# Banded attention stream: value projection moved ahead of the probability transposes

## The chip, the cores and the metric

The kernel runs on one core of one Trainium2 chip. The metric is device time in microseconds (us), lower is better. Four engines compute: TensorE (PE in the rows; PEld are its weight loads), VectorE (DVE), ScalarE (ACT) and GpSimd (POOL); SyncE (SP) issues transfers. Each takes its own instructions in the order in which they are written; between engines only semaphores make one wait for another. TensorE writes its results into eight banks of a memory called PSUM, and VectorE or ScalarE has to move them out before a bank can be written again.

## The reference, cut to what matters

The program is a chain of sixteen layers of different kinds on 2048 tokens of 128 features. The change lies in one of them, which the program runs twice with a retention stage between: a transformer of depth 2 with attention in a band of 64 tokens.

```python
def _layer(x, wqkv, qs, ksc, wo, lg, lb, w1, b1, w2, b2):
    h = shift_token(x)
    q, k, v = jnp.split(h @ wqkv, 3, axis=-1)          # 8 heads of 64
    q = l2norm(q) * qs
    k = l2norm(k) * ksc
    q, k = rotary_xpos(q, k)
    o = local_attention(q, k, v)                        # softmax over a band
    x = x + o @ wo
    h = shift_token(x)
    h = layer_norm(h) * lg + lb
    a, g = jnp.split(h @ w1 + b1, 2, axis=-1)
    x = x + (a * gelu(g)) @ w2 + b2
```

## The kernel before, in words

All values are 32-bit floats. A tile is 128 tokens; the 2048 tokens make 16 tiles, and with two layers the stage handles N = 32 tiles, numbered through. Four tiles make a block of 512 tokens, on which the layer norm and the gated MLP work; there are 8 blocks.

The stage is a software pipeline written out by hand. Each engine has one loop over slots `i = 0, 1, 2, ...`, and in slot `i` several tiles are served, each at another step. On TensorE, slot `i` holds in this order: `turn_qk(i-2)` (L880, 8 transposes of the rotated queries and keys), `project_qk(i)` (L833), an early piece of the MLP or norm (`early`, L943 to L963), `scores(i-2)` (L894 for even tiles, L900 for odd), `project_out(i-4)` (L933), in one slot of four `mean(b)` (L943), `turn_p(i-3)` (L911, 8 transposes of the softmax probabilities in two halves), `project_v(i)` (L868), a late piece of the MLP (`late`), and `values(i-3)` (L926, probabilities times values). The pieces of the MLP go round with r = (i - 8) mod 4, from slot 8 on: r = 0 holds the mean and two `hidden` pieces of the block before, r = 1 the variance and `mlp_out` (L969, three matmuls), r = 2 and r = 3 the gates (L957) and a `hidden` piece (L963). In the first slots, 3 to 7, there is no late piece, and in slots 8 and 9 none either, since no block before exists.

Each output has its PSUM bank: `project_v`, `mean`, `var` and some pieces of the MLP share bank B_V (2); `turn_qk` and `turn_p` share the two banks B_T; the scores have the banks B_S; `values` and `project_out` share B_O.

What the moved calls wait for and who waits for them:

- `turn_p(k)` waits until GpSimd has scaled the probabilities (`p_scaled`, L1142) and ScalarE has emptied B_T (`qk_moved`). ScalarE's `move_p` (L1073, two copies of 128x512) waits for it, and `values` waits for these copies.
- `project_v(k)` waits until bank B_V is free: for VectorE's copy of the tile before (`v_copied`, L1179), and for what the piece of this slot left there. In r = 0 that is `centre` (L1240), VectorE's subtraction of the mean; in r = 2 and r = 3 a ScalarE pass on the gate (L1091, L1099). Its own result is fetched by VectorE (`move_v`, L1179) only in the next slot.
- ScalarE's order in a slot is: `exps(i-3, 1)` (L1063), `move_qk(i-2)` (L1052, L1055), `inverse(i-1)` (L1043, L1045), `square(i)` (L1033), a piece of the norm or the gate (in r = 3 the gelu with two loads of a function table, L1099 to L1103), `move_p(i-3)`, `exps(i-2, 0)`. `scores` waits for `move_qk`, through `window_kt` (L1055).

Of the kernel before, what the change touches and what calls it, by code (L numbers as in the profile page):

```python
# [60 lines left out]
def toks(j, w=W):  # L61
    return slice(j * w, (j + 1) * w)
# [647 lines left out]
def window_attention_stage(K, tag):  # L710
# [4 lines left out]
    N, BLOCKS = DEPTH * TILES, DEPTH * NJ  # L715
# [59 lines left out]
    def part(i):  # L775
        b, r = divmod(i - FIRST, TPW)
        return (b if 0 <= b < BLOCKS else None), (b - 1 if 1 <= b <= BLOCKS else None), r
# [6 lines left out]
    with nc.Block() as block:  # L784
# [35 lines left out]
        def _(pe):  # L820
            def project_qk(k):
                l, j = k // TILES, (k % TILES) // TPW
                if k == 0:
                    pe.wait_ge(st.wa_ready, 16 * DEPTH)
                    pe.wait_ge(outer.norm_ready, 2)
                if k % TPW == 0:
                    pe.wait_ge(sh_ready[j], 32 * (l + 1))
                if k >= 1:
                    pe.wait_ge(st.squared, k)
                    pe.wait_ge(st.cosed, k)  # L830
                    pe.wait_ge(st.sined, 2 * k)
                for a in range(2):
                    mm = nc.tensor.matmul(K.ps[:, B_Q + a, :], sh[:, tok(k)], w_qkv(l, a), start=True, stop=True)  # L833
                mm.then_inc(st.qk_ready, 1)

            def early_moved(i):
                b, last, r = part(i)
                if r == 0 and last is not None:
                    pe.wait_ge(st.hid_done, 3 * last + 2)
                if r == 1 and b is not None:  # L840
                    pe.wait_ge(st.log_ready, b + 1)
                if r >= 2 and b is not None:
                    pe.wait_ge(st.g_moved, 3 * b + 2 * r - 3)

            def mean_moved(i):
                b, last, r = part(i)
                if r == 0 and b is not None:
                    pe.wait_ge(st.centered, b + 1)
# [12 lines left out]
            def project_v(k):  # L861
                if k == 0:
                    pe.wait_ge(outer.norm_ready, 3)
                if k >= 1:
                    pe.wait_ge(st.v_copied, k)
                early_moved(k)
                mean_moved(k)
                nc.tensor.matmul(K.ps[:, B_V, :], sh[:, tok(k)], w_qkv(k // TILES, 2), start=True, stop=True)\  # L868
                    .then_inc(st.v_ready, 1)

            def turn_qk(k):
                if k == 0:
                    pe.wait_ge(outer.log_ready, NJ)
                    pe.wait_ge(outer.norm_ready, NJ)
                pe.wait_ge(st.k_scaled, k + 1)
                if k >= 1:
                    pe.wait_ge(st.pt_copied, 2 * (k - 1))
                for a in range(2):
                    for c in range(QC):
                        mm = nc.tensor.transpose(K.ps[:, B_T + a, toks(c, P)],  # L880
                                                 pa[:, k % 2, a, 2 * c:2 * c + 2, :].rearrange("p h d -> p (h d)"), K.ident)
                    mm.then_inc(st.qk_turned, 1)

            def scores(k):
                pe.wait_ge(st.qk_moved, 2 * (k + 1))
                if k >= 1:
                    pe.wait_ge(st.masked, 2 * k)
                late_moved(k + 1)
                q, keys = (k // 2) % 2, kt[:, (k // 2) % 2]
                for c in range(QC):  # L890
                    if k % 2 == 0:
                        for e in range(2):
                            rows = slice(64 * e, 64 * e + 64)
                            mm = nc.tensor.matmul(K.ps[:, B_S + e, toks(c, P)], qt[rows, c, :], keys[rows, c, 0:P],  # L894
                                                  start=True, stop=True)
                    else:
                        for e in range(2):
                            for u in range(2):
                                rows, own = slice(64 * e, 64 * e + 64), slice(64 * u, 64 * u + 64)
                                mm = nc.tensor.matmul(K.ps[own, B_S + e, toks(c, P)], qt[rows, c, own],  # L900
                                                      keys[rows, c, 64 + 64 * u:64 + 64 * u + P], start=True, stop=True)
                mm.then_inc(st.sim_ready, 1)

            def turn_p(k):
                for e in range(2):
                    pe.wait_ge(st.p_scaled, 2 * k + e + 1)
                    if e == 0:
                        last = min(k + 1, N - 1)
                        pe.wait_ge(st.qk_moved, 2 * (last + 1))
                    for c in range(QC):  # L910
                        mm = nc.tensor.transpose(K.ps[:, B_T + e, toks(c, P)], s[:, k % 2, e, c, :], K.ident)  # L911
                    mm.then_inc(st.pt_ready, 1)
# [17 lines left out]
            def project_out(k):  # L930
                pe.wait_ge(st.o_moved, k + 1)
                for c in range(QC):
                    mm = nc.tensor.matmul(K.ps[:, B_O, 0:P], w_out(k // TILES, c), of[:, c, :],  # L933
                                          start=(c == 0), stop=(c == QC - 1))
                mm.then_inc(st.proj_ready, 1)

            def mean(b):
                l, j = divmod(b, NJ)
                if b < BLOCKS - 1:
                    pe.wait_ge(sh2_ready[j], 32 * (l + 1))  # L940
                else:
                    pe.wait_ge(st.y_attn, N)
                nc.tensor.matmul(K.ps[:, B_V, :], K.mean_mat, sh2[:, toks(j)], start=True, stop=True)\  # L943
                    .then_inc(st.mean_ready, 1)
# [28 lines left out]
            def early(i):  # L973
                b, last, r = part(i)
                pe.wait_ge(st.v_copied, up_to(i))
                if i > N:
                    early_moved(i - 1)
                    mean_moved(i - 1)
                if r == 0 and last is not None:
                    hidden(last, 1)  # L980
                if r == 1 and b is not None:
                    var(b)
                if r == 2 and b is not None:
                    gate(b, 0)
                if r == 3 and b is not None:
                    gate(b, 2)

            def late(i):
                b, last, r = part(i)
                pe.wait_ge(st.masked, up_to(2 * (i - 2) + 1, 2 * N))  # L990
                if i > N + 1:
                    late_moved(i - 1)
                if r == 0 and last is not None:
                    hidden(last, 2)
                if r == 1 and last is not None:
                    mlp_out(last)
                if r == 2 and b is not None:
                    gate(b, 1)
                if r == 3 and b is not None:
                    hidden(b, 0)  # L1000

            outer.pe(pe, 0, K.x, lambda j: None)
            for i in stream:
                b, last, r = part(i)
                if 2 <= i < N + 2:
                    turn_qk(i - 2)
                if i < N:
                    project_qk(i)
                if i >= FIRST:
                    early(i)  # L1010
                if 2 <= i < N + 2:
                    scores(i - 2)
                if 4 <= i < N + 4:
                    project_out(i - 4)
                if r == 0 and b is not None:
                    early_moved(i)
                    mean(b)
                if 3 <= i < N + 3:
                    turn_p(i - 3)
                if i < N:  # L1020
                    project_v(i)
                if i >= FIRST:
                    late(i)
                if 3 <= i < N + 3:
                    values(i - 3)
# [3033 lines left out]
```

## Time and profile before

| | us |
|---|---|
| runs | 2560.93, 2563.16, 2550.03 (median 2560.93) |
| profiled execution | 2562.57 |
| span of the profile | 2560.8 |
| busy in the span: PE | 2188.4 (85%) |
| DVE | 1711.1 (67%) |
| ACT | 1431.7 (56%) |
| POOL | 716.6 (28%) |

The two banded attention stages lie at about 391 to 757 us (first projection to last piece of the MLP) and at about 813 to 1178 us. The shares above are means over sixteen stages with different limits; what this change does has to be read inside these two.

### The profile page before, as it was taken

Reading aid. Unit: us, or ns where it says so; the run is one execution under the profiler, and the core shown is the slowest. Engines: PE = TensorE matmul, PEld = TensorE weight load, DVE = VectorE, ACT = ScalarE, POOL = GpSimd, SP = SyncE. Lnnn points to the kernel's source line nnn. Section 1 sums busy time; section 2 is a strip of 40 time slices with the busy share of each in tenths; the row PEclk is TensorE's granted clock in tenths of the full one; section 3 lists DMA queues with packets and bytes.
Section 4 is the critical chain, followed back from the end, with each engine's and each line's share of the span. In section 5 each row is a group of like instructions: output and inputs, shape, how many; then the busy total and the mean of one; then the engine's idle time right before and its main releaser. Section 6 shows DMA issues by size and latency. Waiting matters only on the chain. (4 is left out here: it accounts for less than half of the span.)

```text
span 2560.8 us, 43202 instructions
## 1 busy us (share of the span) xinstructions
PE 2188.4 (85%) x15324; PEld 1484.8 (58%) x15324; DVE 1711.1 (67%) x4380; ACT 1431.7 (56%) x3703; POOL 716.6 (28%) x473
## 2 busy tenths in 40 slices
PE   5999997999987999998748888768876989889998
PEld 4788774665644656653547774423423767656657
DVE  6777757887846988873655554356455989547874
ACT  3555646777764887876512215563645756235762
POOL 0000004554511654540133420000011879132000
PEclk9999999999998999999868998988986989888998
DMA  1000002011002010101022220000001212100010
GB/s 59 15 14 20 9 26 63 22 28 24 22 14 79 18 28 20 30 18 51 1 65 56 56 47 4 9 12 7 4 13 42 83 66 75 69 12 1 2 69 18
DMA packets 79492, 81.47 MB, mean 32 GB/s; under 512 B 28688, under 2 KB 64272, under 8 KB 78256
## 3 DMA queue, kind: packets, MB, share of 16 engines
q1 hardware_dynamic: 79280, 78.72, 10.7%
q8 instruction: 124, 2.03, 0.3%
q14 instruction: 88, 0.72, 0.1%
HBM read 53.94 MB, written 8.52 MB: 24 GB/s over the span
## 5 line engine op out<-in xcount | busy, mean ns | idle before, releaser
L1142 POOL TENSOR_TENSOR window_s<-window_s,window_soft 128x512 f32<-128x512 f32 x128 | 132.9, 1039 | 301.2 <-DVE window_soft L1172 301.2
L1232 DVE CUSTOM_DVE_ANT_0 window_s<-ps,window_mask,window_nrn 128x128 f32<-128x128 f32 x512 | 148.5, 346 | 95.6 <-PE ps L900 52.2
L1063 ACT ACTIVATE window_s<-window_s,window_soft 128x128 f32<-128x128 f32 x512 | 197.9, 395 | 2.5 <-DVE window_soft L1232 2.5
L3218 DVE TENSOR_TENSOR_SCAN mamba_bx<-ps,mamba_ab 128x256 f32<-128x256 f32 x256 | 154.6, 667 | 20.4 <-PE ps L3004 20.4
L1150 POOL TENSOR_TENSOR window_pa<-window_pa,window_pb 128x1024 f32<-128x1024 f32 x64 | 151.3, 2364 | 39.0 <-DVE window_pb L1214 39.0
L833 PE MATMUL ps<-window_wa,window_sh 128*128 128x512 f32 x256 | 127.3, 621 | 25.8 <-DVE window_pb L1214 14.1
L3388 ACT ACTIVATE rope_p<-ps,rope_mx 128x128 f32<-128x128 f32 (+1 forms) x256 | 104.1, 418 | 50.5 <-DVE rope_mx L3442 50.4
L3001 PE MATMUL ps<-mamba_m,mamba_xt 128*128 128x129 f32 x512 | 102.9, 283 | 29.7 <-ACT mamba_m L3076 20.6
L1073 ACT ACTIVATE window_pt<-ps 128x512 f32<-128x512 f32 x128 | 69.7, 595 | 85.9 <-PE ps L911 85.8
L3106 POOL TENSOR_TENSOR h<-mamba_bx,mamba_cbr 128x1024 f32<-128x1024 f32 x32 | 89.2, 2792 | 96.3 <-DVE mamba_bx L3218 95.7
L83 PE MATMUL ps<-x,consts 128*128 128x512 f32 x120 | 75.3, 786 | 45.7 <-PEq L53 40.1
L580 POOL TENSOR_TENSOR linattn_y<-linattn_y,linattn_wa 128x512 f32<-128x512 f32 x24 | 28.3, 1179 | 303.2 <-DVE linattn_xn L619 303.2
L3076 ACT ACTIVATE mamba_m<-mamba_step,mamba_b_tm 128x129 f32<-128x129 f32 (+1 forms) x256 | 78.4, 389 | 60.6 <-PE ps L3004 57.0
L3001 PEld LDWEIGHTS ps<-mamba_m,mamba_xt 128*128 128x128 f32 x512 | 82.2, 197 | 49.5 <-issue 49.5
L1933 ACT ACTIVATE delta_ym<-ps 128x512 f32<-128x512 f32 x48 | 28.7, 597 | 130.0 <-PE ps L1739 130.0
L3004 PE MATMUL ps<-mamba_m,mamba_xt 128*128 128x128 f32 x512 | 101.1, 279 | 0.0
L1063 ACT ACTIVATION_READ_ACCUMULATOR window_s<-window_s,window_soft 128x1 f32 x512 | 99.6, 194 | 0.0
L417 PE MATMUL ps<-linattn_h,linattn_wb 128*128 128x512 f32 x192 | 95.9, 604 | 1.8 <-ACT linattn_h L493 1.8
L3106 POOL TENSOR_TENSOR ln_xc<-mamba_bx,mamba_cbr 128x1024 f32<-128x1024 f32 x32 | 90.0, 2813 | 22.3 <-DVE mamba_bx L3218 21.3
L3094 POOL MEMSET mamba_xi<- 128x48 f32 x1 | 0.1, 148 | 342.1 <-POOLq L53 342.1
L426 PE MATMUL ps<-linattn_wb,linattn_hid 128*128 128x128 f32 x768 | 89.7, 275 | 0.0
L426 PEld LDWEIGHTS ps<-linattn_wb,linattn_hid 128*128 128x128 f32 x768 | 87.7, 192 | 0.0
(615 smaller groups left out, 6173.2 us busy)
## 6 DMA issues: line engine op xcount, KB each, us to landing
mamba_cbr<-mamba_c SPq DMA_DIRECT2D x32, 512.0 KB, 3.5
window_vs<-window_vt SPq DMA_DIRECT2D x64, 128.0 KB, 2.3
delta_xi<-delta_x SPq DMA_DIRECT2D x16, 512.0 KB, 4.7
switch_w<-in_switch_w SPq DMA_DIRECT2D x4, 2048.0 KB, 10.0
window_wa<-in_window_wa SPq DMA_DIRECT2D x4, 1152.0 KB, 6.6
linattn_wb<-in_linattn_wb SPq DMA_DIRECT2D x6, 513.0 KB, 3.6
window_wb<-in_window_wb SPq DMA_DIRECT2D x4, 537.5 KB, 7.7
window_sh<-y SPq DMA_DIRECT2D x16, 128.0 KB, 3.7
```

The lines of the kernel that those rows point to most:

```text
L417: nc.tensor.matmul(K.ps[:, B_H + c % 2, :], w1(s, c), h[:, 1, s % 2, :], start=True, stop=True)\
L426: mm = nc.tensor.matmul(K.ps[:, B_O, toks(t, P)], hid[:, s % 2, c, toks(t, P)], w2(s, c), start=(c == 0), stop=(c == CH - 1))
L833: mm = nc.tensor.matmul(K.ps[:, B_Q + a, :], sh[:, tok(k)], w_qkv(l, a), start=True, stop=True)
L1063: a = nc.scalar.activation(s[:, k % 2, e, c, :], s[:, k % 2, e, c, :], ACT.Exp, scale=-1.0, bias=soft[:, k % 2, e, 1, c:c + 1], accum_out= ...
L1142: nc.gpsimd.tensor_tensor(s[:, k % 2, e], s[:, k % 2, e], soft[:, k % 2, e, 3, :].unsqueeze(2).to_broadcast([P, QC, P]), ALU.mult)\
L1150: nc.gpsimd.tensor_tensor(own, own, pb[:, :, :, :].rearrange("p a h d -> p (a h d)"), ALU.add)\
L1232: v = nc.vector.tensor_tensor_reduce(s[:, k % 2, e, c, :], K.ps[:, B_S + e, toks(c, P)], mask[:, k % 2, :], nrn[:, k % 4, h:h + 1], 3e38, ...
L3001: nc.tensor.matmul(out[:, at0:at0 + P + 1], xt[:, TH * H + 2 * q, toks(c, P)], m[:, (k // CC) % 2, 2 * q, :], start=(q % 2 == 0), stop=Fal ...
L3004: mm = nc.tensor.matmul(out[:, at0 + P:at0 + LEN], xt[:, TH * H + 2 * q + 1, toks(c, P)], m[:, (k // CC) % 2, 2 * q + 1, 0:P], start=False ...
L3106: nc.gpsimd.tensor_tensor(cg_buf(k), g_buf(k), cbr[:, (k // CC) % 4, :], ALU.mult).then_inc(st.cg_ready, 1)
L3218: g = nc.vector.tensor_tensor_scan(g_buf(k)[:, LEN * q:LEN * (q + 1)], K.ps[:, v_bank(k) + q // 2, at0:at0 + LEN], a_buf(k)[:, LEN * q:LEN ...
L3388: a = nc.scalar.activation(p[:, n % 2, e, part_of(t)], K.ps[:, 2 * (n % 2) + e, part_of(t)], ACT.Exp, bias=mx[:, n % 4, t, e:e + 1], accum ...
```

## The change

`project_v(i)` and `turn_p(i - 3)` change places in TensorE's loop. Nothing is added or removed, and the other four engines' instructions stand as before. `turn_p` runs in slots 3 to 34 and `project_v` in slots 0 to 31, so the order changes in slots 3 to 31: 29 slots in each of the two stages.

```diff
                 if r == 0 and b is not None:
                     early_moved(i)
                     mean(b)
+                if i < N:
+                    project_v(i)
                 if 3 <= i < N + 3:
                     turn_p(i - 3)
-                if i < N:
-                    project_v(i)
                 if i >= FIRST:
                     late(i)
```

The first place is on TensorE in slot 5 of the first stage, before the MLP has begun. `window_of` is the attended output that `project_out` reads, `window_s` the probabilities, `window_sh` the shifted input, `window_pt` the transposed probabilities. Before:

```order
L900 MATMUL ps<-window_kt,window_qt 64x128 x16
L933 MATMUL ps<-window_of,window_wa 128x128 x4
L911 MATMUL ps<-consts,window_s 128x128 x8
L868 MATMUL ps<-window_wa,window_sh 128x512
L926 MATMUL ps<-window_pt,window_vt 64x128 x8
```

and after:

```order
L900 MATMUL ps<-window_kt,window_qt 64x128 x16
L933 MATMUL ps<-window_of,window_wa 128x128 x4
L868 MATMUL ps<-window_wa,window_sh 128x512
L911 MATMUL ps<-consts,window_s 128x128 x8
L926 MATMUL ps<-window_pt,window_vt 64x128 x8
```

The projection (L868) no longer stands between the transposes (L911) and the product that needs their copies (L926).

The second place is on TensorE in a slot with r = 0, where the mean of a block (L943, of `window_sh2`, which the names show as `window_sh`) goes into bank B_V. Before:

```order
L894 MATMUL ps<-window_kt,window_qt 128x128 x8
L933 MATMUL ps<-window_of,window_wa 128x128 x4
L943 MATMUL ps<-window_sh,consts 128x512
L911 MATMUL ps<-consts,window_s 128x128 x8
L868 MATMUL ps<-window_wa,window_sh 128x512
L963 MATMUL ps<-ln_xc,window_wb 85x512
L926 MATMUL ps<-window_pt,window_vs 64x64 x2
```

and after:

```order
L894 MATMUL ps<-window_kt,window_qt 128x128 x8
L933 MATMUL ps<-window_of,window_wa 128x128 x4
L943 MATMUL ps<-window_sh,consts 128x512
L868 MATMUL ps<-window_wa,window_sh 128x512
L911 MATMUL ps<-consts,window_s 128x128 x8
L963 MATMUL ps<-ln_xc,window_wb 85x512
L926 MATMUL ps<-window_pt,window_vs 64x64 x2
```

The transposes no longer stand between the two matmuls that use bank B_V, L943 and L868.

## Rows read from the trace of the kernel before

**Rows 1.** Page, part 1: busy us, share of the span, instructions.

```profile
PE 2188.4 (85%) x15324; PEld 1484.8 (58%) x15324; DVE 1711.1 (67%) x4380; ACT 1431.7 (56%) x3703; POOL 716.6 (28%) x473
```

**Rows 2.** Busy us by stretch: PE, PEld, DVE, ACT, POOL; granted clock, DMA share, GB/s.

```profile
520.00:560.00 40.00, 37.84 (x325) 24.45 (x322) 32.81 (x111) 31.56 (x99) 19.81 (x15) 1.00 0.09 20
```

**Rows 3.** Waits of PE, 822 to 1140 us: total us, times, longest.

```profile
PE ps L926 <- ACT window_pt L1073: 7.8, 6, 1.3
...
PE ps L943 <- DVE window_hid L1257: 5.1, 6, 0.9
...
PE ps L963 <- DVE window_vt L1179: 0.4, 1, 0.4
PE ps L957 <- DVE window_vt L1179: 0.4, 1, 0.4
```

**Rows 4.** Timeline of PE, one block: start us, us, what, [idle before <-releaser].

```profile
521.50 1.04 PE L911 MATMUL ps<-consts,window_s 128*128 128x128 f32 x8
522.38 1.02 PE L868 MATMUL ps<-window_wa,window_sh 128*128 128x512 f32 x2
523.24 1.02 PE L957 MATMUL ps<-ln_xc,window_wb 128*128 128x512 f32 x2
524.19 0.34 PE L926 MATMUL ps<-window_pt,window_vs 128*64 128x64 f32 x4
...
528.87 1.10 PE L900 MATMUL ps<-window_kt,window_qt 64*64 64x128 f32 x32
...
534.97 1.09 PE L926 MATMUL ps<-window_pt,window_vt 128*64 128x128 f32 x16 [1.30 <-ACT window_pt L1073]
...
542.70 1.13 PE L943 MATMUL ps<-window_sh,consts 128*128 128x512 f32 x2 [0.85 <-DVE window_hid L1257]
543.66 1.04 PE L911 MATMUL ps<-consts,window_s 128*128 128x128 f32 x8
544.71 1.10 PE L868 MATMUL ps<-window_wa,window_sh 128*128 128x512 f32 x2
545.64 1.02 PE L963 MATMUL ps<-ln_xc,window_wb 128*85 128x512 f32 x2
546.59 0.34 PE L926 MATMUL ps<-window_pt,window_vs 128*64 128x64 f32 x4
...
555.04 2.74 PE L969 MATMUL ps<-window_hid,window_wb 128*128 128x512 f32 x6
```

**Rows 5.** Timeline of ACT in the same block, slots r = 2 and r = 3.

```profile
522.14 1.08 ACT L1073 ACTIVATE window_pt<-ps 128x512 f32<-128x512 f32 x2 [1.31 <-PE ps L911]
...
527.23 0.58 ACT L1055 ACTIVATE window_kt<-ps 128x512 f32<-128x512 f32 x1
528.11 0.22 ACT L1043 ACTIVATE window_stat<-window_stat 128x16 f32<-128x16 f32 x1 [0.29 <-DVE window_stat L1188]
...
533.83 1.08 ACT L1073 ACTIVATE window_pt<-ps 128x512 f32<-128x512 f32 x2
```

**Rows 6.** Timeline of DVE in the slot r = 0: the centring.

```profile
543.88 0.68 DVE L1240 TENSOR_TENSOR ln_xc<-window_sh,ps 128x512 f32<-128x512 f32 x1
```

**Rows 7.** Timeline of PE, slots 6 to 8 of the first stage.

```profile
440.77 1.16 PE L894 MATMUL ps<-window_kt,window_qt 64*128 64x128 f32 x16
...
442.86 1.04 PE L911 MATMUL ps<-consts,window_s 128*128 128x128 f32 x8
...
446.02 1.09 PE L880 MATMUL ps<-consts,window_pa 128*128 128x128 f32 x8 [0.18 <-POOL window_pa L1154]
...
448.80 1.10 PE L900 MATMUL ps<-window_kt,window_qt 64*64 64x128 f32 x32
...
461.28 1.10 PE L868 MATMUL ps<-window_wa,window_sh 128*128 128x512 f32 x2 [0.48 <-DVE ln_xc L1240]
```

**Rows 8.** Timeline of ACT, slots 6 and 7 of the first stage.

```profile
443.49 1.08 ACT L1073 ACTIVATE window_pt<-ps 128x512 f32<-128x512 f32 x2 [0.68 <-PE ps L911]
...
448.02 0.58 ACT L1055 ACTIVATE window_kt<-ps 128x512 f32<-128x512 f32 x1
```

## The prediction, made before the changed kernel was run

> **What bounds the kernel now.** I read from wide to narrow. The page's first part has TensorE busy for 85% of the whole span [rows 1], which says little about two stages out of sixteen. The busy time by stretch says more: in the repeating part of the banded stage TensorE works 37.84 of 40 us, at full granted clock (2.4 GHz), while VectorE works 32.81 and ScalarE 31.56 [rows 2]. So TensorE's order is the time there, and whatever makes it stand still is added. The view of waits then says where it stands still already [rows 3]: in six slots `values` waits 1.3 us each for ScalarE's copies of the probabilities (L1073), in six slots the mean waits 0.85 us for VectorE, and only twice, 0.4 us each, does a piece wait for VectorE's copy of the projected values. The wait that the new order could remove, transposes (L911) waiting for GpSimd with a projection idle behind them, has no row in this stretch. The timelines give the distances [rows 4 to 8].
>
> **The change part by part.** Both calls stay, so TensorE's work is the same: a slot of 0.88 us for the transposes (521.50 to 522.38) and 0.86 us for the projection (522.38 to 523.24) [rows 4]. What changes is who stands behind whom. Three things follow.
>
> First, the transposes come 0.86 us later, and with them ScalarE's two copies. From the start of the transposes to the start of the copies it takes 522.14 - 521.50 = 0.64 us, the copies take 1.08, and `values` starts 0.06 behind them (533.83 + 1.08 = 534.91, start at 534.97) [rows 4, 5]. So `values` can't begin earlier than 1.78 us after the transposes begin. Before, the projection and the late piece stood between and covered that: 524.19 - 521.50 = 2.69 us. Now what covers it is the transposes (0.88) and the late piece alone (524.19 - 523.24 = 0.95), together 1.83 us. In a slot with a late piece that is just enough, with 0.05 us left: I take 0 and keep 0 to 0.1. In r = 1 the late piece is `mlp_out` (2.74 us) and covers everything.
>
> Slots 3 to 7 have no late piece. There I follow the round of two engines, from scores to the next scores. Scores to transposes is 442.86 - 440.77 = 2.09 us, transposes to the end of ScalarE's copy of the keys is 448.02 + 0.58 - 442.86 = 5.74 us (copies, eight exponentials and the copies of queries and keys, back to back), and 0.06 for the semaphore: 7.89 us, hidden under a period of 448.80 - 440.77 = 8.03 us that another chain sets, through GpSimd [rows 7, 8]; the 0.18 us that L880 waits for it there is the mark of that. With the projection between scores and transposes the round becomes 7.89 + 0.86 = 8.75 us and sets the period: +0.72 us. Slot 3 still has waits that swallow it; four periods follow, so 4 x 0.72 = 2.9 us. Bounds: 0 if the copies are covered after all, 4 x 0.86 = 3.4 if nothing is.
>
> Second, bank B_V. In r = 0 the mean (L943) and the projection both write it, and VectorE must centre in between. Centring starts at 543.88, directly when VectorE is free, and ends at 544.56; the projection starts at 544.71 [rows 4, 6]. That time is set by VectorE and doesn't move when the projection is put earlier in the queue. Before, the transposes filled it (543.66 to 544.54). Now TensorE stands still from 543.66 to 544.71, and the transposes start at 545.64 behind the projection. They end at 546.52, the late piece at 547.47, against 546.59 for the start of `values` before: +0.88 us. The copies are ready at 545.64 + 1.78 = 547.42, in time. This happens in slots 12, 16, 20, 24 and 28: 5 x 0.88 = 4.4 us. The bounds are 0 (if centring came so much earlier that nothing waits) and 1.05 us each, the whole new gap. Slot 8 is the same without a late piece: the projection starts at 461.28 as before [rows 7], the transposes take the place that `values` had behind it, and `values` comes 1.78 us later. It used to come about 0.1 us after the projection, so I take 1.7 us, between 0.9 and 1.8. In slot 9, also without a late piece, what follows waits 0.40 us for VectorE's copy of the values (L957) [rows 3] behind other VectorE-set starts, so the 0.86 is swallowed there: 0, at most 0.86.
>
> The Trainium skill has a rule against such a neighbourhood: "Perfetto Trace Analysis", section Matmuls, wants independent matmul groups to rotate through different PSUM banks so that the evacuation of one overlaps the next group's matmuls. The new order puts two users of one bank side by side in r = 0 and takes away the group from another bank. By this rule alone only the slots with a mean would pay; the rows agree that they pay and say that others do too.
>
> Third, ScalarE's lateness. In r = 2 its copies start at 522.14 after 1.31 us of idling, and from there to the key copy, which ends at 527.81, nothing is idle; the next gap is 0.29 us before L1043 at 528.11 [rows 5]. Shift it all by 0.86: the key copy ends at 528.67, still before the scores at 528.87 [rows 4], but L1043 and all behind it come 0.86 - 0.29 = 0.57 us later. What follows is the chain of two table loads and gelus, without a gap, up to the copies at 533.83, and these are what `values` waits for in r = 3, 1.30 us now, 1.87 us then. Six slots (11, 15, ..., 31): 6 x 0.57 = 3.4 us; bounds 0 (another gap that I don't see in the chain) and 0.86. The other effect of the order in r = 3 is free: the projection must wait for the gate pass of ScalarE (L1099), but TensorE waits for ScalarE later in that slot anyway.
>
> What the earlier projection itself can win: VectorE fetches it in the next slot and isn't waiting for it, so the most is the two waits for that copy, 0.8 us a stage [rows 3]. I take 0, since VectorE comes to it at its own time.
>
> Sum for one stage: 2.9 + 1.7 + 4.4 + 3.4 = 12.4 us. A delay once made is not won back, as each next step hangs on `values` or `scores`, and the stage ends at a barrier. Twice: 24.8 us. The profiled execution took 2562.57 us, 1.6 us above the median of the three; from there 2587.4, from the median of 2560.93 it is 2585.7. I say 2586.
>
> **The rivals.**
>
> A, only the bank pair costs. The copies are late in no slot that matters, ScalarE catches up before the gelus; left are the six slots with a mean, (4.4 + 1.7) x 2 = 12.2 us, 2573. For it: that gap is the plainest in the rows. Against it: ScalarE's rows show no idle time in which to catch up.
>
> B, every slot pays. If the 0.05 us of cover in slots with a late piece isn't there (`mlp_out` aside), and what is late adds to itself through ScalarE, the bound is 29 x 0.86 x 2 = 50 us, 2611. For it: 0.05 us is less than the rows can promise. Against it: only the missing part of the cover would be paid, not the whole 0.86.
>
> C, not slower, by one mechanism: in r = 3 TensorE waits 1.30 us for ScalarE. If that chain starts from something that doesn't move with TensorE, the 0.88 us lost in r = 0 comes out of this wait instead of being added, and the third part is 0 too. Left is the start, (2.9 + 1.7) x 2 = 9.2 us, 2570, which is within 0.5%; it decides itself at the point where a block's loss is under 1.30 us. With the start swallowed as well it is 2561. Against it: the chain starts at L1043, which waits for VectorE, and VectorE in its turn for the scores of TensorE.
>
> D, faster: the value copies come sooner and the two waits of 0.4 us go, 2 x 0.8 = 1.6 us, 2559; anything more would need a wait of the transposes for GpSimd, and there is none to fill.
>
> **How the numbers follow.** The forecast has 0.62, A 0.12, B 0.06, C 0.16, D 0.04. About 0.5%, or 12.8 us, is what a measurement of this kernel can tell from no change, since its three runs lie 13 us apart. Slower by more than that, above 2573.7: the forecast, B and a part of A, 0.76; within it: the rest of A and C, 0.20; faster 0.04. The forecast's own range is 2575 to 2598 (below, the third part at 0, 6.8 us less, and some of the start; above, 0.86 in the third part and in slot 9, and a part of the cover missing). For 8 in 10 I go down to 2568, which takes in A and a part of C, and up to 2600.
>
> **What the next profile would show.** In r = 0, L943 followed by a gap of about 1 us before L868, released by VectorE's L1240, then L911. In r = 3, the wait of `values` for L1073 near 1.9 us in place of 1.30. In slots 4 to 7, a period near 8.75 us, with PE waiting for `window_kt` (L1055) and no longer for GpSimd. In slot 8, `values` waiting about 0.9 us for L1073. Each block of four slots, from one wait of `values` in r = 3 to the next, would be 0.88 + 0.57 = 1.45 us longer. I am wrong if the block's length doesn't change, if `values` waits in r = 2 as well, or if busy times of single instructions differ.

## The result, and the profile of the changed kernel

The changed kernel takes 2585.11 us (median of 4 runs, 2578.45 to 2594.75), the kernel before, run beside it, 2559.28 us (4 runs, 2550.03 to 2563.16). The ratio is 1.0104 with an interval of 1.0083 to 1.0125: slower by 1.0%. The prediction was 2586. The profiled executions took 2586.16 and 2562.57 us, 23.6 us apart.

The instruction counts are as before, and the busy times nearly so: on TensorE 2195.2 us in place of 2188.4 [rows 1], the other three compute engines within 3.1 us. First the page's first part, then busy time by stretch (PE, PEld, DVE, ACT, POOL, granted clock, DMA share, GB/s), the same 40 us as [rows 2]:

```profile
PE 2195.2 (85%) x15324; PEld 1486.2 (58%) x15324; DVE 1712.0 (66%) x4380; ACT 1428.7 (55%) x3703; POOL 716.2 (28%) x473
```

```profile
520.00:560.00 40.00, 36.73 (x306) 23.02 (x306) 30.52 (x105) 29.26 (x85) 21.76 (x16) 1.00 0.12 28
```

At the same clock TensorE works 36.73 us there, before 37.84. The two windows don't hold the same pieces of a block. Over the whole stretch that is measured at the end of this section (one stage, from slot 4 on) TensorE is busy for 308.7 us of 341.2, before 306.8 of 328.8, at granted clock 1.00 in both: 10.5 us of the 12.4 are standing still. The other 1.9 us are busy time. A pair of 128x512 matmuls is shown as 1.10 us long behind a wait and as 1.02 in the flow, so part of it belongs to the new waits too. Where TensorE stands still, the view of TensorE's waits shows for the second stage, 822 to 1160 us (total us, times, longest):

```profile
PE ps L868 <- ACT window_gl L1099: 6.7, 6, 1.1
...
PE ps L926 <- ACT window_pt L1073: 6.2, 11, 0.7
PE ps L868 <- DVE ln_xc L1240: 5.8, 6, 1.3
...
PE ps L943 <- DVE window_hid L1257: 5.1, 6, 0.9
...
PE ps L894 <- ACT window_kt L1055: 0.5, 2, 0.4
...
PE ps L963 <- DVE window_vt L1179: 0.4, 1, 0.4
PE ps L868 <- ACT window_gl L1091: 0.2, 1, 0.2
```

The projection (L868), which waited once before, for 0.5 us, now waits thirteen times in this list. The list leaves out waits under 0.15 us, and it says where TensorE stood, not what it cost: some of these waits only took the place of others. TensorE's timeline over one block (start us, us, what, [idle before <-releaser]) answers to [rows 4]:

```profile
525.45 1.04 PE L911 MATMUL ps<-consts,window_s 128*128 128x128 f32 x8
526.32 1.02 PE L957 MATMUL ps<-ln_xc,window_wb 128*128 128x512 f32 x2
527.28 0.34 PE L926 MATMUL ps<-window_pt,window_vs 128*64 128x64 f32 x4
...
531.96 1.10 PE L900 MATMUL ps<-window_kt,window_qt 64*64 64x128 f32 x32
...
535.27 1.10 PE L868 MATMUL ps<-window_wa,window_sh 128*128 128x512 f32 x2 [1.11 <-ACT window_gl L1099]
536.20 1.04 PE L911 MATMUL ps<-consts,window_s 128*128 128x128 f32 x8
537.07 1.02 PE L963 MATMUL ps<-ln_xc,window_wb 128*128 128x512 f32 x2
538.52 1.09 PE L926 MATMUL ps<-window_pt,window_vt 128*64 128x128 f32 x16 [0.42 <-ACT window_pt L1073]
...
546.25 1.12 PE L943 MATMUL ps<-window_sh,consts 128*128 128x512 f32 x2 [0.85 <-DVE window_hid L1257]
548.26 1.10 PE L868 MATMUL ps<-window_wa,window_sh 128*128 128x512 f32 x2 [0.89 <-DVE ln_xc L1240]
549.19 1.04 PE L911 MATMUL ps<-consts,window_s 128*128 128x128 f32 x8
550.06 1.02 PE L963 MATMUL ps<-ln_xc,window_wb 128*85 128x512 f32 x2
551.02 0.34 PE L926 MATMUL ps<-window_pt,window_vs 128*64 128x64 f32 x4
...
582.77 1.09 PE L926 MATMUL ps<-window_pt,window_vt 128*64 128x128 f32 x16 [0.42 <-ACT window_pt L1073]
```

The block, from `values` in r = 3 to the next, lasts 582.77 - 538.52 = 44.25 us; before it was 577.89 - 534.97 = 42.92, from the row in [rows 4] to this one:

```profile
577.89 1.09 PE L926 MATMUL ps<-window_pt,window_vt 128*64 128x128 f32 x16 [1.30 <-ACT window_pt L1073]
```

In r = 2 `values` starts 527.28 - 525.45 = 1.83 us after the transposes without waiting: the cover holds. In r = 0 it starts 551.02 - 546.25 = 4.77 us after the mean, before 3.89 [rows 4]. In r = 3 it starts 538.52 - 531.96 = 6.56 us after the scores, before 6.10.

ScalarE's timeline, slots r = 2 and r = 3, answers to [rows 5]:

```profile
526.09 1.09 ACT L1073 ACTIVATE window_pt<-ps 128x512 f32<-128x512 f32 x2 [2.18 <-PE ps L911]
...
531.18 0.59 ACT L1055 ACTIVATE window_kt<-ps 128x512 f32<-128x512 f32 x1
531.66 0.22 ACT L1043 ACTIVATE window_stat<-window_stat 128x16 f32<-128x16 f32 x1
...
537.38 1.08 ACT L1073 ACTIVATE window_pt<-ps 128x512 f32<-128x512 f32 x2
```

L1043 no longer waits for VectorE; it starts 0.30 us before the scores (531.96 - 531.66) in place of 0.76 (528.87 - 528.11). That 0.46 us is what `values` loses in r = 3.

In the first slots TensorE's timeline answers to [rows 7]:

```profile
434.89 1.09 PE L926 MATMUL ps<-window_pt,window_vt 128*64 128x128 f32 x16 [0.74 <-ACT window_pt L1073]
...
438.92 1.16 PE L894 MATMUL ps<-window_kt,window_qt 64*128 64x128 f32 x16 [0.19 <-ACT window_kt L1055]
...
443.65 0.34 PE L926 MATMUL ps<-window_pt,window_vs 128*64 128x64 f32 x4 [0.74 <-ACT window_pt L1073]
...
447.67 1.10 PE L900 MATMUL ps<-window_kt,window_qt 64*64 64x128 f32 x32
...
460.86 1.10 PE L868 MATMUL ps<-window_wa,window_sh 128*128 128x512 f32 x2 [1.34 <-DVE ln_xc L1240]
```

The period is 447.67 - 438.92 = 8.75 us where it was 8.03. L880 no longer waits for GpSimd; the scores of slot 6 wait 0.19 us for the key copy.

For the whole stage I measure from the start of the scores in slot 4 to the start of the last `mlp_out`. In the first stage this is 753.55 - 424.74 = 328.8 us before and 762.71 - 421.48 = 341.2 after, +12.4; in the second it is the same to 0.1 us. Twice 12.4 is 24.8 us. The profiled executions differ by 1.2 us less; that difference lies outside these stretches.

### The profile page after: what moved, and what is told of

Read it like the earlier page. It is cut to its first block and busy times, and to the rows that moved or that the text cites. A ratio compares the mean times of both kernels' runs of the same rounds, so it can differ in the third digit from the quotient of the medians.

```text
span 2584.4 us, 43202 instructions
## 1 busy us (share of the span) xinstructions
PE 2195.2 (85%) x15324; PEld 1486.2 (58%) x15324; DVE 1712.0 (66%) x4380; ACT 1428.7 (55%) x3703; POOL 716.2 (28%) x473
## 5 line engine op out<-in xcount | busy, mean ns | idle before, releaser
L1073 ACT ACTIVATE window_pt<-ps 128x512 f32<-128x512 f32 x128 | 69.7, 595 | 142.4 <-PE ps L911 142.3
L833 PE MATMUL ps<-window_wa,window_sh 128*128 128x512 f32 x256 | 127.1, 621 | 21.8 <-DVE window_pb L1214 12.3
L868 PE MATMUL ps<-window_wa,window_sh 128*128 128x512 f32 x128 | 69.9, 629 | 25.4 <-ACT window_gl L1099 13.4
```

## The experiments

The first six start from the kernel before, the last two from the changed one. The first four were run beside a kernel before of 2556.76 us (median of 25 runs), the last four beside one of 2559.18 (23 runs). One execution of each was profiled, and the rows come from it. Three lines more in the source turn L1073, L1099 and L1240 into L1076, L1102 and L1243 there (in the fifth L1079, L1105 and L1246; in the eighth nothing moves). "Stretch" is slot 4's scores to the last `mlp_out`, 328.8 us before.

**1. New order in r = 0 alone.**

```diff
+                ahead = i >= FIRST and r == 0
+                if i < N and ahead:
+                    project_v(i)
                 if 3 <= i < N + 3:
                     turn_p(i - 3)
-                if i < N:
+                if i < N and not ahead:
                     project_v(i)
```

> The new order only in the slots with r = 0 (slot 8, 12, 16, 20, 24, 28), the old one elsewhere. Theory: the projection waits there for the centring of bank B_V, and nothing behind wins it back. Each block of four slots grows by 0.88 us (from 42.9), slot 8 costs 1.7 us, in all (5 x 0.88 + 1.7) x 2 = 12.2 us over the kernel before; the wait of values for ScalarE's copies in r = 3 stays at 1.30 us. Rival (C of the prediction): the 0.88 us comes out of that wait, which falls to about 0.4 us, the block keeps its length, and only slot 8 costs, 3.4 us in all. Rival: only lateness of ScalarE's copies costs, then the block is unchanged and its wait too.

Measured: 2574.15 us against 2556.76, ratio 1.0073 (1.0052 to 1.0094). In TensorE's timeline the wait in r = 3 stays:

```profile
538.39 1.09 PE L926 MATMUL ps<-window_pt,window_vt 128*64 128x128 f32 x16 [1.30 <-ACT window_pt L1076]
546.11 1.13 PE L943 MATMUL ps<-window_sh,consts 128*128 128x512 f32 x2 [0.85 <-DVE window_hid L1260]
548.13 1.10 PE L868 MATMUL ps<-window_wa,window_sh 128*128 128x512 f32 x2 [0.89 <-DVE ln_xc L1243]
...
582.18 1.09 PE L926 MATMUL ps<-window_pt,window_vt 128*64 128x128 f32 x16 [1.30 <-ACT window_pt L1076]
```

This block lasts 43.79 us, +0.87, and slot 8 costs 1.7 us. Rival C falls: nothing is taken out of the 1.30 us. Four of the ten slots with a mean (12 to 28, in both stages) cost 1.68 us more, and there the timeline looks like this:

```profile
500.64 1.12 PE L943 MATMUL ps<-window_sh,consts 128*128 128x512 f32 x2 [0.85 <-DVE window_hid L1260]
502.65 1.93 PE L868 MATMUL ps<-window_wa,window_sh 128*128 128x512 f32 x2 [0.89 <-DVE ln_xc L1243]
504.38 1.91 PE L911 MATMUL ps<-consts,window_s 128*128 128x128 f32 x8
```

The two matmuls take 1.93 us in place of 1.10. The busy time by stretch has the granted clock (third number from the end) in the same place, where before it was 1.00:

```profile
500.00:510.00 10.00, 8.47 (x57) 5.20 (x58) 7.25 (x19) 4.27 (x17) 2.14 (x3) 0.83 0.00 0
```

This is a mean over 10 us; between 503 and 505 us the same view gives 0.50, which is 1.2 GHz. Together that is 12.2 + 4 x 1.68 = 18.9 us by the trace, 17.4 by the medians. The expectation was right on the mechanism and 5 us short on the whole. In the profiled execution the clock accounts for it. That execution was the slowest of the four (2582.51 us, the others 2572.09 to 2575.54), and what the clock did in the others isn't on record.

**2. New order in slots 3 to 7 alone** (`ahead = 3 <= i < FIRST`).

> The new order only in slots 3 to 7, where no late piece stands between transposes and values. Theory: the round scores, projection, transposes, copies, exponentials, key copy, scores becomes 8.72 to 8.75 us and sets the period in place of 8.03; 4 x 0.7 = 2.8 to 2.9 us a stage, 5.7 us in all; values waits 0.74 us for L1073 in each of these slots and the wait of L880 for GpSimd goes. Rival: the 0.74 us of waiting is only moved from other waits and the period stays at 8.03, 0 us.

Measured: 2562.90 us, ratio 1.0023 (1.0012 to 1.0033), 6.1 us more than before. The periods are 8.75, 8.69, 8.75 and 8.74 us, before 8.03, 8.01, 8.03 and 8.02; the stretch is 331.7 us, +2.9, and blocks stay at 42.92. The round through ScalarE sets the period, as expected.

**3. New order in r = 2 alone** (`ahead = i >= FIRST and r == 2`).

> The new order only in slots with r = 2. Theory: in the slot itself TensorE loses nothing, but ScalarE is about 0.86 us late from its copies on, catches up 0.3 to 0.4 us, and brings the gelus of r = 3 and the copies behind them 0.46 to 0.57 us late: the wait of values in r = 3 grows from 1.30 to 1.76 to 1.87 us, the block by as much, 6 x 0.5 x 2 = 5.5 to 6.8 us in all. Rival: ScalarE catches up before the gelus; the wait stays at 1.30 us, the block at 42.9, 0 us.

Measured: 2566.96 us, ratio 1.0040 (1.0023 to 1.0056). TensorE's timeline in r = 2 and r = 3:

```profile
521.63 1.04 PE L911 MATMUL ps<-consts,window_s 128*128 128x128 f32 x8
522.51 1.02 PE L957 MATMUL ps<-ln_xc,window_wb 128*128 128x512 f32 x2
523.46 0.34 PE L926 MATMUL ps<-window_pt,window_vs 128*64 128x64 f32 x4
...
531.45 1.10 PE L868 MATMUL ps<-window_wa,window_sh 128*128 128x512 f32 x2 [0.24 <-ACT window_gl L1102]
532.38 1.02 PE L963 MATMUL ps<-ln_xc,window_wb 128*128 128x512 f32 x2
534.70 1.09 PE L926 MATMUL ps<-window_pt,window_vt 128*64 128x128 f32 x16 [1.30 <-ACT window_pt L1076]
```

The block is 578.08 - 534.70 = 43.38 us, +0.46. In these slots the order in one slot is paid in the next, in which nothing was changed. The sign I named was wrong: the wait of `values` stays at 1.30 us and the lateness shows in front of the projection, which now waits for L1102. It starts 3.31 us after the scores, before 2.90; the view counts only 0.24 of that as idle. Slot 10 costs 0.44 us of its own and slot 30 another 0.27: their gate pass (L1091) is still running when the projection comes. The stretch is 332.3 us, +3.5, so 7.0 us for both stages. The medians differ by 10.2 us. The ten runs spread from 2560.04 to 2575.61 us, and the profiled one, 2560.50, is near their lower end; what the slower ones did isn't shown.

**4. New order in r = 3 alone** (`ahead = i >= FIRST and r == 3`).

> The new order only in slots with r = 3. In the changed kernel the projection waits 1.11 us there for ScalarE's gate pass (L1099). Theory: that wait costs nothing, since values later in the slot waits for ScalarE in any case; with the new order in r = 3 alone the projection waits about 0.65 us and values about 0.65 us in place of 1.30, the block stays at 42.9 us, 0 us in all. Rival: the wait for L1099 is a cost of its own, 0.6 us or more for each of six slots, 7 us or more in all.

Measured: 2559.34 us, ratio 1.0004 (0.9990 to 1.0018); block 576.61 - 533.69 = 42.92 us, stretch 328.8.

```profile
530.44 1.10 PE L868 MATMUL ps<-window_wa,window_sh 128*128 128x512 f32 x2 [0.65 <-ACT window_gl L1102]
533.69 1.09 PE L926 MATMUL ps<-window_pt,window_vt 128*64 128x128 f32 x16 [0.42 <-ACT window_pt L1076]
```

So 0.65 of the 1.11 us that the projection waits for L1099 in the changed kernel (head of its list, 6.7 us) costs nothing. The other 0.46 is the lateness from r = 2, which the third experiment has shown to cost.

**5. In r = 0: transposes, mean, late piece, projection, values.**

```diff
+                around = i < N and r == 0 and last is not None
+                if around:
+                    turn_p(i - 3)
                 if r == 0 and b is not None:
                     early_moved(i)
                     mean(b)
-                if 3 <= i < N + 3:
+                if around:
+                    late(i)
+                    project_v(i)
+                if 3 <= i < N + 3 and not around:
                     turn_p(i - 3)
-                if i < N:
+                if i < N and not around:
                     project_v(i)
-                if i >= FIRST:
+                if i >= FIRST and not around:
                     late(i)
```

> The kernel before, with another order in slots 12, 16, 20, 24 and 28 alone: transposes, mean, late piece, projection, values, in place of mean, transposes, projection, late piece, values. Theory: the transposes fill the 0.85 us in which the mean waits for VectorE, and the late piece (0.95 us, another bank) fills the time in which bank B_V is centred. The projection then starts as before, and values comes right behind it, 0.95 us sooner: block 42.92 - 0.95 = 41.97 us, 5 x 0.95 x 2 = 9.5 us faster than before. Rival: the next wait for VectorE or ScalarE (the 1.30 us in r = 3) takes the time back, 0 us.

Measured: 2551.53 us against 2559.18, ratio 0.9969 (0.9955 to 0.9984): faster than both kernels. The view shows no wait of TensorE in r = 0 any more; below TensorE's rows stands the centring on VectorE:

```profile
538.88 1.04 PE L911 MATMUL ps<-consts,window_s 128*128 128x128 f32 x8
539.90 1.12 PE L943 MATMUL ps<-window_sh,consts 128*128 128x512 f32 x2
540.86 1.02 PE L963 MATMUL ps<-ln_xc,window_wb 128*85 128x512 f32 x2
541.91 1.10 PE L868 MATMUL ps<-window_wa,window_sh 128*128 128x512 f32 x2
542.94 0.34 PE L926 MATMUL ps<-window_pt,window_vs 128*64 128x64 f32 x4
...
541.09 0.68 DVE L1246 TENSOR_TENSOR ln_xc<-window_sh,ps 128x512 f32<-128x512 f32 x1
```

The block is 574.23 - 532.17 = 42.06 us, -0.86, and the stretch 324.5, -4.3: 8.6 us for both stages, where 9.5 was expected. `values` directly behind the projection starts 542.94 - 541.91 = 1.03 us after it, where the expectation had 0.93 (L868 to L963 in [rows 4]); that is the 0.09 us a block that are missing. The projection itself starts 5.11 us after the slot's scores, before 5.12, and 0.14 us behind the end of the centring (541.77): it still goes by VectorE. It starts 1.05 us after L963, where two such pieces without a wait stand 0.86 us apart (L868 and L957 in [rows 4]), so up to 0.2 us of waiting is left, which the view doesn't show.

**6. In r = 0: transposes ahead of the mean, the rest as before** (the fifth without its middle part).

> The kernel before, with the transposes ahead of the mean in slots 12, 16, 20, 24 and 28, and then projection, late piece and values as before. Theory: the transposes fill the mean's wait of 0.85 us, and the same time comes back as a gap of about 0.9 us before the projection, which waits for the centring: block 42.92 us, 0 us. Rival: filling the wait of 0.85 us is a gain of its own, 5 x 0.85 x 2 = 8.5 us faster.

Measured: 2558.41 us, ratio 0.9998 (0.9980 to 1.0015); block 42.92 us, stretch 328.8. The mean's wait is gone and L868 waits 0.89 us for the centring (L1243). One wait filled with the work that filled the other: no change. It was the late piece, put where the transposes had stood, that made the fifth faster. The late piece moved without the transposes wasn't run.

**7. The changed kernel, with the old order in r = 2** (`ahead = not (i >= FIRST and r == 2)`).

> The changed kernel with the old order put back in slots with r = 2 alone (10, 14, ..., 30). Theory: what r = 3 loses comes from ScalarE's lateness that begins in r = 2, so the part of 0.46 us a block goes and 0.88 us for the centring stays: block 43.80 us in place of 44.25, and slot 10 gets its 0.44 us back; (0.44 + 6 x 0.46) x 2 = 6.4 us less than the changed kernel, 18 us over the kernel before. In r = 3 the projection waits 0.66 us for L1099 and values 0.42 us for L1073. Rival: the loss in r = 3 comes from the order in r = 3 itself; then the block stays at 44.25 us.

Measured: 2585.56 us, ratio 1.0099 (1.0077 to 1.0121). Blocks at full clock last 585.12 - 541.32 = 43.80 us, so the part of r = 2 has gone; in r = 3 L868 waits 0.65 us and L926 0.42. Yet the median is only 1.4 us under that of the changed kernel (2586.95, eighth experiment) and not 6.4: in three slots with a mean the clock falls as in the first experiment, 3 x 1.68 = 5.0 us. The two stretches, 341.2 and 339.5 us, are 1.8 us shorter together than the changed kernel's; without the three falls it would be 6.9.

**8. The changed kernel again.**

> The changed kernel once more, for its granted clock. With the new order in r = 0 alone the clock fell to 1.2 GHz four times behind the gap before L868; in the first profile of the changed kernel it fell nowhere in the repeating blocks. Expected if the drop is a matter of where the gaps happen to lie: blocks of 44.25 us again, each drop, if there are any, making one block about 1.7 us longer, and times between 2578 and 2595 us. Rival: the changed kernel never drops there, and its runs spread no more than those of before.

Measured: 2586.95 us (4 runs, 2586.26 to 2589.30), ratio 1.0109 (1.0087 to 1.0131). The blocks last 44.25 us, the stretch 341.3 us, and no slot from 4 on in either stage is at the lower clock. The rival holds for this profile; it can't say what the run of 2594.75 us did.

## Why the prediction was right, point by point

The terms, for one stage, against the distances between the scores of one slot and the next:

| term | predicted us | measured us | how measured |
|---|---|---|---|
| slots 4 to 7 | 2.9 | 2.85 | 34.93 - 32.08, four periods |
| slot 8 | 1.7 | 1.73 | 11.89 - 10.16 |
| slot 9 | 0 | 0 | 9.51 and 9.52 |
| slot 10 | 0 | 0.44 | 9.89 - 9.45 |
| r = 0, five slots | 4.4 | 4.4 | 5 x (12.56 - 11.68) |
| r = 3, six slots | 3.4 | 2.76 | 6 x (11.18 - 10.72); slot 31: 10.58 - 10.12 |
| slot 30 | 0 | 0.27 | 9.73 - 9.46 |
| sum | 12.4 | 12.4 | 341.2 - 328.8 |

- **TensorE's order is the time there.** Right: the slots not named in the table keep their lengths to 0.01 us, so no delay was won back. The stretch starts at slot 4; that slot 3 swallows its part can't be read, since the slots before it differ by more than 0.7 us between profiles (slot 2 of the second stage lasts 7.83 us before and 9.26 after).
- **Copies not covered in slots 3 to 7.** Right in mechanism and size (second experiment), with both signs: the wait for L1055 came (one row of 0.2 us a stage) and the one for GpSimd went.
- **Cover of 0.05 us in r = 2 and r = 1.** It held in every slot with a late piece, and rival B falls; `values` never waits there.
- **Slots 8 and 9.** Right. In slot 8 `values` waits 0.79 us (0.9 was said); the view names no releaser, but ScalarE's copies end at 463.51 and `values` starts at 463.62. In slot 9 `values` comes 0.85 us later (4.71 us after the scores, before 3.86), and L957 starts 8.46 us after them in both: the VectorE-set starts between swallow it. Only about 0.1 us of that slack is left, so the 0 was near its limit.
- **Bank B_V.** Right (first experiment). The rule of the Trainium skill, "Perfetto Trace Analysis", Matmuls, that independent groups should rotate through different PSUM banks, agrees with the trace: L868 waits 0.89 us behind the mean in the same bank, and in the fifth experiment, with a late piece of another bank between, at most 0.2. Taken alone, as the prediction says, it leads to rival A, 12.2 us, half of what was lost.
- **ScalarE late from r = 2 to r = 3.** Right in mechanism (third, fourth and seventh experiments), too large by 0.11 us a slot. I took ScalarE's slack as the 0.29 us of idling in the row of L1043. But L1043 can start 0.48 us after the key copy (531.18 to 531.66), ahead of that copy's end, and before it started 0.88 us after (527.23 to 528.11): the slack was 0.40, and 0.86 - 0.40 = 0.46.
- **Missed.** Slots 10 and 30, the first and the last with r = 2. In the slots between, ScalarE's gate pass (L1091) starts 0.73 us after the scores and is done when the projection comes. In slot 10 it starts at 1.62 and in slot 30 at 1.46 us, and the projection starts behind its end, 2.45 and 2.28 us after the scores in place of 2.09:

```profile
480.26 1.10 PE L868 MATMUL ps<-window_wa,window_sh 128*128 128x512 f32 x2 [0.20 <-ACT window_gl L1091]
...
701.82 1.10 PE L868 MATMUL ps<-window_wa,window_sh 128*128 128x512 f32 x2
```

I had looked at one block in the middle and took it for all. These 0.71 us a stage were left out, and the term for r = 3 was 0.64 too large. That the two offset each other, so that the sum agrees to 0.1 us, is luck; the mechanisms and the other terms are not.
- **The sign for r = 3.** I expected `values` to wait 1.87 us for L1073; it waits 0.42 and the projection 1.11 for L1099. I had written that the projection would wait there, and then left it out of the sign. Where two waits follow each other, the first takes from the second: here 1.11 and 0.42 us in place of 0 and 1.30.
- **Rival D.** VectorE's copy of the values came no sooner, and L963's wait of 0.4 us for it stayed; that of L957 in slot 9 went, since TensorE came later there and L957 started no sooner.

## What to carry to other kernels

In a hand-written order on an engine that hardly rests, an operation is also the cover of the one before it: before moving it, ask for each neighbour how long its result takes to come back, and what is left in between. Neighbours that write one bank want work of another bank between them (here the transposes ahead of the mean and the late piece behind it, 8.6 us together, and nothing for the transposes alone). Judge a new wait by the distance between two fixed points on the busy engine, and not by its length: of the longest wait of the changed kernel more than half cost nothing, and one slot's order was paid in the next. Look at the first and the last round of a loop too, and not at one in the middle.

## What the runs showed of the hardware that was not expected

TensorE's granted clock fell from 2.4 to 1.2 GHz inside the repeating blocks, where the kernel before stays at the upper level: in four of ten slots with a mean in the first experiment's profile (12 and 24 of the first stage, 16 and 28 of the second), in three of ten in the seventh's (12, 24 and 20), where TensorE had waited 0.85 and 0.89 us with one matmul pair between. Each fall made the slot 14.24 - 12.56 = 1.68 us longer. The same two waits stand in every block of the changed kernel, and in none of the twenty in its two profiles did the clock fall. What decides it between blocks that look alike was not settled. In the profiled executions it is why two kernels whose blocks differ by 0.45 us took nearly the same time (2585.53 and 2587.25 us).
